# Spreading six merged low-rank parts over the first six down products of a slot

## The reference

```
weights = router(x)                                   # (tokens, 8 experts)
gate = x @ Wg[e];  up = x @ Wu[e]                     # 512 -> 512, per expert
gate[:2] += x @ Ga @ Gb;  up[:2] += x @ Ua @ Ub       # low rank, R = 64, experts 0 and 1 only
mid = silu(gate) * up
out = mid @ Wd[e];  out[:2] += mid @ Da @ Db
y = sum_e weights[e] * out[e]
```

## Time and profile before

| | |
|---|---|
| median of 3 runs | 2319.34 us (2316.86 to 2319.48) |
| profiled execution, its own time | 2319.87 us |
| its span | 2318.2 us |
| mean granted clock of PE | 0.992 |
| PE, DVE, ACT, POOL busy | 97%, 68%, 38%, 33% |
| mean DMA traffic | 67 GB/s |

### The profile page before, as it was taken

The page is one execution under the profiler, slowest core; times in us unless marked ns, Lnnn a source line. Parts: engine busy times, 40 slices in busy tenths (PEclk is TensorE's granted clock), DMA queues, the critical chain, the costliest instruction groups (busy, mean ns, idle before and its releaser), DMA issues.

```text
span 2318.2 us, 30910 instructions
## 1 busy us (share of the span) xinstructions
PE 2257.0 (97%) x10746; PEld 1863.4 (80%) x10746; DVE 1582.3 (68%) x2394; ACT 891.1 (38%) x1455; POOL 766.6 (33%) x585
## 2 busy tenths in 40 slices
PE   8999999999999999999999899999999999999998
PEld 7887788888878888888877787878778778888886
DVE  5557777777778755683446776867677887666665
ACT  5456333333343222322232543534344444444443
POOL 0003544444413222342111523424233533333332
PEclk9999999999999999999999999999999999999999
DMA  6856222222150100000000122222011021111110
GB/s 210 230 153 185 64 73 72 72 72 72 55 200 15 37 19 19 23 1 19 1 1 28 64 73 91 73 82 82 28 55 55 28 91 55 54 54 54 54 36 37
DMA packets 93224, 155.95 MB, mean 67 GB/s; under 512 B 6576, under 2 KB 56752, under 8 KB 86848
## 3 DMA queue, kind: packets, MB, share of 16 engines
q1 hardware_dynamic: 93120, 154.59, 20.4%
HBM read 115.25 MB, written 39.32 MB: 67 GB/s over the span
## 4 chain that ended last, share of the span: by engine, by line
PE 62%; DVE 5%; issue 2%; ACT 1%; POOL 1%; DVEq 0%; POOLq 0%; ACTq 0%
PE attn_pvk L1235 4%; PE attn_pvk L1236 4%; PE attn_pvk L1237 4%; PE attn_pq L1235 2%; PE attn_pq L1236 2%; PE attn_pq L1237 2%; PE attn_po L1235 2%; PE attn_po L1236 2%; PE attn_po L1237 2%; PE attn_pv L1235 2%; PE attn_pv L1236 2%; PE attn_pv L1237 2%; PE attn_pv L85 2%; PE attn_pv L87 2%; PE attn_pv L86 2%
## 5 line engine op out<-in xcount | busy, mean ns | idle before, releaser
L2720 DVE TENSOR_TENSOR moe_a_lo<-moe_up_raw,moe_a_hi 128x512 fp32r<-128x512 f32 x192 | 183.3, 970 | 147.6 <-ACT moe_a_hi L2153 147.5
L2020 POOL TENSOR_TENSOR moe_h_lo<-moe_c_t,moe_h_hi 128x512 fp32r<-128x512 f32 x96 | 128.5, 1339 | 351.8 <-ACT moe_h_hi L2153 351.8
L1235 PE MATMUL attn_pvk<-moe_b_hi,moe_a_hi 128*128 128x512 f32 x512 | 201.5, 393 | 10.8 <-ACT moe_c_last L2300 7.0
L1237 PE MATMUL attn_pvk<-moe_b_hi,moe_a_lo 128*128 128x512 f32 x512 | 200.3, 391 | 0.0
L1236 PE MATMUL attn_pvk<-moe_b_lo,moe_a_hi 128*128 128x512 f32 x512 | 200.2, 391 | 0.0
L2153 ACT ACTIVATE moe_c_t<-attn_pvk 128x512 f32<-128x512 f32 x192 | 112.8, 595 | 175.9 <-PE attn_pvk L1237 174.1
L1349 POOL TENSOR_TENSOR ffn_h_lo<-ffn_h_f,ffn_h_hi 128x512 fp32r<-128x512 f32 x64 | 92.9, 1453 | 240.1 <-ACT ffn_h_hi L1416 240.1
L1593 DVE SCALAR_TENSOR_TENSOR all_acc<-attn_pvk,ffn_wts,all_acc 128x512 f32<-128x512 f32 x128 | 91.1, 749 | 93.3 <-PE attn_pvk L87 88.3
L2219 ACT ACTIVATE moe_c_t<-moe_c_t 128x512 f32<-128x512 f32 x96 | 60.4, 629 | 241.4 <-DVE moe_c_t L2802 241.3
L2153 ACT ACTIVATE moe_a_hi<-moe_up_raw 128x512 fp32r<-128x512 f32 x192 | 116.0, 624 | 56.4 <-POOL moe_up_raw L1990 56.4
L1235 PEld LDWEIGHTS attn_pvk<-moe_b_hi,moe_a_hi 128*128 128x128 f32 x512 | 96.6, 189 | 34.8 <-issue 8.9
(11 more groups left out here) (526 smaller groups left out, 6579.7 us busy)
## 6 DMA issues: line engine op xcount, KB each, us to landing
moe_up_raw<-in_e_up SPq DMA_DIRECT2D x28, 1024.0 KB, 6.1
moe_dn_raw<-in_e_dn SPq DMA_DIRECT2D x28, 512.0 KB, 3.7
xh<-mix_out_hi SPq DMA_DIRECT2D x32, 256.0 KB, 2.6
zs<-mix_out_z SPq DMA_DIRECT2D x32, 256.0 KB, 3.5
xl<-mix_out_lo SPq DMA_DIRECT2D x32, 256.0 KB, 3.9
mix_x<-xh SPq DMA_DIRECT2D x16, 512.0 KB, 4.1
mix_x<-xl SPq DMA_DIRECT2D x16, 512.0 KB, 5.2
mix_z_raw<-zs SPq DMA_DIRECT2D x16, 512.0 KB, 3.9
```

Of the source, the lines that this page charges most:

```text
L1235: pe.matmul(out, lh, rh, start=first, stop=False, skip_group_check=True)
L1237: return pe.matmul(out, ll, rh, start=False, stop=True, skip_group_check=True)
L2020: tt(h_lo[:, m, tok], src, raw(h_hi[:, m, tok]), ALU.subtract).then_inc(s_hlo, 1)
L2720: tt_(a_lo[q][:], src, raw(a_hi[q][:]), ALU.subtract).then_inc(s_alo, 1)
```

## The change

It alters the placing of m0 to m5 and one of the waits. Before, m0 stood ahead of d0, m1 and m2 ahead of d1, m3 ahead of d2, m4 and m5 ahead of d3. Now one part stands ahead of each of d0 to d5. `merged(n)` follows: the sixth part is now the item 11 of the ring in its slot, and was item 9. A new count `merged_up(n)`, at m3 (item 7), is what POOL's first weight sum and ACT's copy of part 0 wait for. SP's stores, ACT's `down_high` and the loads of the next low-rank factors still use `merged`.

```
         def extra(n, c):
             if at(n, *MERGING):
-                return (1, 3, 4, 6, 6, 6, 6, 6)[c]
+                return (1, 2, 3, 4, 5, 6, 6, 6)[c]
...
         def merged(n):
-            return ring_of(n - 1) + 9
+            return ring_of(n - 1) + 11
+
+        def merged_up(n):
+            return ring_of(n - 1) + 7
...
             def weight_sums(n, par, turn, part):      # POOL
                     if at(n, *LORA):
-                        pool.wait_ge(s_free, merged(n))
+                        pool.wait_ge(s_free, merged_up(n))
...
             def up_high(n, par, turn, q):             # ACT, q == 0
                     if at(n, *LORA):
-                        act.wait_ge(s_free, merged(n))
+                        act.wait_ge(s_free, merged_up(n))
...
             def extras(n, c):                         # PE, and the same on VectorE
                 if at(n, *MERGING):
-                    for j in ((0,), (1, 2), (3,), (4, 5), (), (), (), ())[c]:
+                    for j in ((0,), (1,), (2,), (3,), (4,), (5,), (), ())[c]:
                         merge(n + 1, j)
```

## The result

The changed kernel is slower: 2327.17 us median (7 runs) against 2318.23 us (7 runs), a ratio of 1.0041 with the interval 1.0032 to 1.0051. Measured once more on another occasion it came to 2330.30 against 2316.92, 1.0056 (1.0042 to 1.0070). So it costs some 9 to 13 us. The forecast was 12 us, 2331.3, with a range from 2322 to 2335. It was counted from 2319.34, the median of the first three runs of the kernel before.

The account below looks back on a forecast made before the run. PE, busy for 97% of the span, was taken to bound the kernel; 2.8 + 14.1 + 5.0 - 9.9 gave +12.0 us, so 2331.3 against 2319.34, with a range of 2322 to 2335.

Parts of the forecast that it names:

- The stalls that go: In the merging slots, PE's waits behind m1 and m2 (7.4 us) and slot 5's behind c_last (1.1) vanish.
- T: End of the fifth pair of up products (q4) of a merging slot, from which the prediction counts times.
- m4 and m5 at T: After q4, m4, d4, m5, d5 share a ring of two banks: 0.7 us a slot lost, 2.8 in all.
- The stores: SP's stores wait for m5 and issue at T + 3.7; POOL's sum moves from T + 2.15 to T + 9.5.
- The pauses of d0: PE's d0 in slots 4, 8, 5, 9 waits for h_lo or d7: 4.6, 4.1, 3.9, 1.5, together 14.1 us.
- The clock: PE runs at its lower clock after the pauses of slots 4, 8 and 5: 1.7 us each, 5.0 in all.
- The rival in which the clock holds: PE's clock does not drop after most pauses of d0: +7.0 us, 2326.3; chance 0.18.
- The sum: Whole kernel: 2.8 + 14.1 + 5.0 - 9.9 = +12.0 us, 2331.3 against 2319.34; chance 0.52.
- The turns: POOL's operations and VectorE's four L2720 copies alternate at the SBUF port, some 1.75 us a pair.
- the rival without turns: Late POOL run holds VectorE up no more than now: d0 waits 0.5, 0, 3.0, 0.4; -3.2 us, 2316; chance 0.11.
- the stores are off the path: POOL's sum starts by about T + 7; stalls go, only 2.8 us come: -7.1, 2312; chance 0.05.
- The backlog at the next slot's start: VectorE is late in the next slot too, and slot 9's pause costs clock: 3 to 6 us more, 2336; chance 0.14.

Follow-up runs that it names:

- the first experiment: Changed kernel with the up store issued when m3 is out, on its own semaphore, ahead of the low-rank loads: 2311.14 us, 0.9975 against the kernel before.

## Why the prediction was right

The sign, the range and the mechanism held. That the total came out so close owes something to errors that cancel, as the pauses show. Point by point, for the profiled execution:

**The stalls that go.** 7.4 us behind double merges and the one of c_last: gone. T of slot 3, counted from m0's start (1378.74 to 1397.06), is 18.3 us, and 1399.0 - 1380.78 = 18.2 by the prediction.

**m4 and m5 at T.** 0.7 us a slot forecast, 0.66 measured (0.36 at m5, 0.30 in restarts and d5).

**The stores.** T + 3.7 forecast and measured. POOL's sum (now L1990) at T + 9.5 forecast, T + 9.2 measured, as the stores landed 5.5 and not 5.8 us after their issue.

**The pauses of d0.** Forecast 4.6, 3.9, 4.1 and 1.5 us for slots 4, 5, 8 and 9; measured with one restart 4.0, 4.8, 3.8 and 1.3, 13.9 in all against 14.1. Slot 5 was 0.9 us longer, as slot 4's stores took 7.1 us to L1990 (1441.59 to 1448.66) and not 6.1; the other three were 0.6, 0.3 and 0.2 shorter. The closeness of the sum is luck in so far.

**The clock.** 5.0 us forecast for three pauses. What is left of 20.9 after 2.6 and 13.9 is 4.4: about 1.5 a pause and not 1.7, and all three lost it. In the second profile of the changed kernel the pauses are the same, 13.9 us, and the clock costs 5.3. The rival in which the clock holds did not happen in any run here with such pauses.

**The sum.** +12.0 forecast; +10.9 and +11.9 in this stretch of the two traces, +8.9 and +13.4 us by the medians of the two measurements. The single item most mis-sized is the pause of slot 5, by 0.9 us; of the terms of the sum it is the price of the clock, 0.6 us too high against the first trace and 0.3 too low against the second.

**The rivals.** The turns are shown (copies of 1.76 us, each ending after the POOL operation beside it). The waits that the prediction gives for the rival without turns stand in the order of slots 4, 8, 5 and 9. That the stores are off the path is refuted by the trace (POOL waits for them until T + 9.2) and by the first experiment: only when an edit takes the up store off the path does the gain come, 6.0 us where 7.1 was reckoned, the 1.4 us of d0 in slots 4 and 8 being left. The backlog at the next slot's start was there, but hidden behind the pause of d0; the run with d7 out first brought it to light. What the prediction did not say is that all of VectorE's backlog, and not d7's place in it or one POOL operation more or less, sets when slots 4 and 8 go on; the forecast did not need it, the experiments on d7 and `h_lo` missed for want of it.

## What to carry to other kernels

When a count of "all parts are done" moves because its last part moves, look up everyone who awaits it: relaxing it for the consumers (here ACT and POOL) does nothing for a copy-out (here SP's store) that must finish before the next engine may overwrite the tile. Give each tile its own condition, and its own semaphore where two transfers share one. An order of work is then worth judging: the same new order was 9 to 13 us slower with the shared condition and 6 us faster with separate ones. And where an engine has fallen behind, moving one of its results ahead can only move the place at which the others wait for it: here d7 ahead of the copies turned a wait of d0 into one of m1.

## What the runs showed of the hardware that was not expected

**The turns hold through a whole queue.** VectorE's copies with two SBUF inputs took 1.7 to 1.8 us each, and not 0.68, three in a row behind a first of 1.23 in the changed kernel and four in a row (1.66 to 1.79) with d7 out first, as long as POOL had work queued. Moving one POOL operation out of the queue left the four unchanged. The Trainium skill, SBUF – State Buffer ("Who interferes with whom"), has the exclusion for a whole instruction; the trace agrees and adds that neither engine kept the port for two instructions in these rows.

**The clock fell after shorter pauses than I had counted.** With the first `h_lo` ahead, a pause of 2.65 us in slot 5 was followed 1.3 us later by steps of 0.43 us, at a granted clock of 0.50; with d7 out first, one of 1.92 us in slot 4 by six such steps, and one of the same length in slot 8 as well. In the kernel before, pauses of 0.94 and 0.46 us were followed by none.

**The same pause does not always cost the same.** In two profiles of the changed kernel the pause of slot 5 is 4.5 us, but the slow steps behind it end at 1459.15, 3.0 us after PE resumed, in the one and at 1461.16, 4.8 us after, in the other: 1.35 us lost and 2.2. PE's rows in the second profile:

```profile
1456.34 0.76 PE L1235 MATMUL attn_pv<-moe_dn_hi,moe_h_hi 128*128 128x512 f32 x1 [4.54 <-issue]
...
1461.16 0.40 PE L1237 MATMUL attn_pt<-moe_b_hi,moe_a_lo 128*128 128x512 f32 x1
```

**One kernel, two measurements.** The changed kernel measured 1.0041 and 1.0056 against the same kernel before, 3.1 us apart in the median. Differences below some 4 us between two of these kernels are not settled here.
